# Output tiles at the end of a slot, and the exponentials' bias on ScalarE

## The reference

```python
q = hidden_states @ _dequant(q_codes, q_scales)
k = hidden_states @ _dequant(k_codes, k_scales)
v = hidden_states @ _dequant(v_codes, v_scales)
...
q = _rope(q)
k = _rope(k)
k = jnp.repeat(k, rf, axis=1)
v = jnp.repeat(v, rf, axis=1)
scores = jnp.einsum('bhqd,bhkd->bhqk', q, k) * scale + mask[None, None]
attn = jax.nn.softmax(scores, axis=-1)
out = jnp.einsum('bhqk,bhkd->bhqd', attn, v)
out = out.transpose(0, 2, 1, 3).reshape(b, s, NH * HD)
return out @ _dequant(o_codes, o_scales)
```

## Time and profile before

| what | us |
|---|---|
| median of 3 runs | 1576.78 |
| lowest and highest of them | 1571.9, 1584.11 |
| the profiled execution | 1574.17 |
| its span in the profile | 1572.4 |

### The profile page before, as it was taken

The page is one execution under the profiler, slowest core; times in us unless marked ns, Lnnn a source line. Parts: engine busy times, 40 slices in busy tenths (PEclk is TensorE's granted clock), DMA queues, the critical chain, the costliest instruction groups (busy, mean ns, idle before and its releaser), DMA issues.

```text
span 1572.4 us, 40997 instructions
## 1 busy us (share of the span) xinstructions
PE 1443.0 (92%) x11104; PEld 852.1 (54%) x11104; DVE 1294.1 (82%) x2884; ACT 926.2 (59%) x2198; POOL 935.1 (59%) x642
## 2 busy tenths in 40 slices
PE   4778899999999999999999999999999976999998
PEld 2445555556655555555565555556555553544543
DVE  7866689998889898889988999899889885776744
ACT  2465566667667666666667666666666762322421
POOL 2566677777777776777777777777777752110100
PEclk8989899999999999999999999999999987999999
DMA  8379988889889889988888888888988774010000
GB/s 265 61 165 178 166 154 158 158 157 165 158 156 162 155 160 155 167 154 161 158 171 162 163 161 155 161 160 161 166 158 156 142 130 91 14 54 29 26 28 27
DMA packets 522616, 217.15 MB, mean 138 GB/s; under 512 B 478944, under 2 KB 480704, under 8 KB 522432
## 3 DMA queue, kind: packets, MB, share of 16 engines
q1 hardware_dynamic: 519968, 210.53, 70.0%
q0 software_dynamic: 2464, 4.23, 1.5%
HBM read 55.32 MB, written 4.19 MB: 38 GB/s over the span
## 4 chain that ended last, share of the span: by engine, by line
PE 41%; issue 15%; DVE 11%; SPq 11%; DMA 10%; POOL 6%; ACT 4%; DVEq 2%; POOLq 0%; ACTq 0%
DMA ot<-o_parts 6%; DVE prob L1127 4%; SPq L384 4%; PE ps_s L1023 4%; PE ps_s L1024 4%; POOL p_lo L504 4%; PE ps_p L812 3%; PE ps_p L813 3%; PE ps_p L788 3%; PE ps_p L790 3%; PE ps_p L789 3%; DMA swap<-other 2%; PE ps_p L1037 2%; PE ps_p L1038 2%; DVE y L1114 2%
## 5 line engine op out<-in xcount | busy, mean ns | idle before, releaser
L504 POOL TENSOR_TENSOR p_lo<-prob,p_hi 128x1280 f16<-128x1280 f32 x128 | 340.7, 2661 | 175.8 <-ACT p_hi L633 155.5
L1114 DVE SCALAR_TENSOR_TENSOR y<-ps_p,wo_scale,y 128x512 f32<-128x512 f32 x512 | 380.8, 745 | 53.3 <-PE ps_p L813 31.6
L624 ACT ACTIVATE prob<-prob,exp_bias 128x512 f32<-128x512 f32 (+3 forms) x512 | 283.1, 553 | 164.7 <-DVE exp_bias L1136 164.3
L812 PE MATMUL ps_p<-ot,wo 128*128 128x512 f16 x512 | 199.5, 390 | 74.6 <-DMA ot<-o_parts 59.8
L788 PE MATMUL ps_p<-x_hi,w_hi 128*128 128x512 f16 x640 | 245.3, 383 | 5.5 <-DVE w_lo L1048 3.4
L789 PE MATMUL ps_p<-x_lo,w_hi 128*128 128x512 f16 x640 | 244.9, 383 | 0.0
L790 PE MATMUL ps_p<-x_hi,w_lo 128*128 128x512 f16 x640 | 244.7, 382 | 0.0
L1127 DVE CUSTOM_DVE_ANT_0 prob<-ps_s,mask 128x512 f32<-128x512 f32 (+3 forms) x512 | 237.0, 481 | 8.4 <-PE ps_s L827 7.3
L841 PE MATMUL ps_o<-v_hi,ffn_w 128*128 128x128 f16 x1280 | 222.6, 220 | 11.6 <-DVE rot L1102 11.0
L488 POOL TENSOR_TENSOR rot<-rot,swap 128x512 f32<-128x512 f32 x160 | 202.4, 1273 | 46.1 <-DMA swap<-other 45.8
L842 PE MATMUL ps_o<-v_lo,ffn_w 128*128 128x128 f16 x1280 | 222.4, 220 | 0.0
(11 more groups left out here) (100 smaller groups left out, 2979.7 us busy)
## 6 DMA issues: line engine op xcount, KB each, us to landing
swap<-other SPq DMA_DIRECT2D x320, 128.0 KB, 3.0
w_code<-w_codes SPq DMA_DIRECT2D x36, 384.0 KB, 3.7
w_scale<-w_scales SPq DMA_DIRECT2D x36, 384.0 KB, 4.9
o_code<-o_codes SPq DMA_DIRECT2D x35, 256.0 KB, 3.1
swap<-x SPq DMA_DIRECT2D x16, 256.0 KB, 2.8
out<-z SPq DMA_DIRECT2D x16, 256.0 KB, 2.0
ffn_w<-x SPq DMA_DIRECT2D x3, 1024.0 KB, 9.8
ffn_w<-p_hi SPq DMA_TRANSPOSE x128, 3.6
```

What stands on the lines that cost most here:

```text
L504: pool.tensor_tensor(p_lo[:, :], prob[:, hp, :], p_hi[:, :], ALU.subtract).then_inc(p_lod, 1)
L624: act.activation(prob[:, hp, a:a + w], prob[:, hp, a:a + w], ACT.Exp, bias=exp_bias[:, hp, i:i + 1], scale=-1.0, accum_out=exp_sum[:, hp, ...
L812: pe.matmul(ps_p[:, bank, :], w, flat(ot[:, hp, 0:TT, :]), start=True, stop=False)
L1114: dve.scalar_tensor_tensor(tile, ps_p[:, bank, :], scale, tile, ALU.mult, ALU.add).then_inc(o_add, 1)
```

## The change

Three things. The four output tiles of a slot go behind all scores and all pieces, on PE and on DVE, and V goes ahead of Q2. The bias is made by ACT, one instruction for each group of scores, ahead of that group's exponentials, with a wait for its own result. On POOL rope_add moves ahead of o_low, and on ACT v_high moves ahead of the last group of exponentials. Lines of the changed kernel are numbered a little differently (output tiles 818 and 819, attend 847 to 849).

```diff
-FULL = (("K",), ("Q0", "Q1"), ("Q2", "V"), ("Q3",))
+FULL = (("K",), ("Q0", "Q1"), ("V", "Q2"), ("Q3",))
...
-START = ("K", "Q0", "Q1", "Q2", "V", "Q3")
+START = ("K", "Q0", "Q1", "V", "Q2", "Q3")
...
 def slot_sequence(pieces):
-    return ("O0", "O1", "O2") + pieces + ("O3",)
+    return pieces + ("O0", "O1", "O2", "O3")
...
             def exps(n, hp, g):
+                first, count = min(GROUPS[g]), len(GROUPS[g])
+                act.wait_ge(low_done, n * TT + DONE[g])
+                act.activation(exp_bias[:, hp, first:first + count], low[:, hp, first:first + count], ACT.Copy,
+                               bias=EXP_UP).then_inc(bias_done, 1)
+                act.wait_ge(bias_done, n * NG + g + 1)
                 for i in GROUPS[g]:
                     a, w = P_AT[i], (i + 1) * P
-                    act.wait_ge(bias_done, n * NG + g + 1)
...
                     if more:
-                        scores(*nxt, 0)
-                    out_tile(n, h, 0)
-                    if more:
-                        scores(*nxt, 1)
-                    out_tile(n, h, 1)
-                    if more:
-                        scores(*nxt, 2)
-                    out_tile(n, h, 2)
+                        for g in range(NG):
+                            scores(*nxt, g)
                     for piece in slots[h]:
...
-                    out_tile(n, h, 3)
+                    for nt in range(KT):
+                        out_tile(n, h, nt)
...
                         if more:
                             lows(n + 1, hp, g)
-                            bias(n + 1, hp, g)
-                        out_tile(h, g)
...
                     for V, vpar, piece, bank, taken in made(U, r, h, slots):
-                        if piece != "V":
-                            take(V, vpar, piece, bank, taken)
-                    out_tile(h, 3)
-                    for V, vpar, piece, bank, taken in made(U, r, h, slots):
-                        if piece == "V":
-                            take(V, vpar, piece, bank, taken)
+                        take(V, vpar, piece, bank, taken)
+                    for nt in range(KT):
+                        out_tile(h, nt)
```

More of the change, by code:

```diff
@@ L541, in unit @@
                     p_low(n, h % 2)
+                    roped = [x for x in made_before(U, r, h, slots) if x[2] != "V"]
+                    if first and h == 0:
+                        start_rope("Q3")
+                    else:
+                        for V, vpar, piece, bank, taken in roped:
+                            rope_add(V, vpar, piece, taken)
                     if not (first and h < 2):
@@ L544, in unit @@
                     if first and h == 0:
-                        start_rope("Q3")
                         rope_low(0, 0, "Q3")
                     else:
-                        roped = [x for x in made_before(U, r, h, slots) if x[2] != "V"]
-                        for V, vpar, piece, bank, taken in roped:
-                            rope_add(V, vpar, piece, taken)
                         for V, vpar, piece, bank, taken in roped:
@@ L663, in _ @@
             rope_high(0, 0, "K")
+            v_high(0, 0, START.index("V") % 2, START.index("V") + 1)
             xt_high(2)
@@ L669, in _ @@
             o_centre(0)
-            v_high(0, 0, START.index("V") % 2, START.index("V") + 1)
             rope_high(0, 0, "Q1")
@@ L708, in unit @@
                                 rope_high(V, vpar, piece)
+                    for V, vpar, piece, bank, taken in made(U, r, h, slots):
+                        if piece == "V":
+                            v_high(V, vpar, bank, taken)
                     if more:
@@ L711, in unit @@
                         p_high(n + 1, (h + 1) % 2)
-                    for V, vpar, piece, bank, taken in made(U, r, h, slots):
-                        if piece == "V":
-                            v_high(V, vpar, bank, taken)
                     for piece in slots[h]:
@@ L1129, in lows @@
                                              accum_out=low[:, hp, i:i + 1]).then_inc(low_done, 1)
[L1131 to L1137, removed]
             def invert(n, h):
@@ L1172, in _ @@
                 lows(0, 0, g)
-                bias(0, 0, g)
             start_piece(5)
```

## The result

| | us |
|---|---|
| before, median of 4 runs | 1574.93 (1571.9 to 1584.11) |
| after, median of 4 runs | 1667.31 (1659.32 to 1671.28) |
| ratio, 95% interval | 1.057 [1.051, 1.063] |
| profiled execution after, its span | 1667.43, 1665.6 |

The account below looks back on a forecast made before the run. PE, busy 92%, was taken to bound the kernel. The unit was to grow from 38.24 to 40.02 us, +50 over 28 units, start -5, so 1574 + 45 = 1619 us; range 1572 to 1652.

Parts of the forecast that it names:

- I credit the whole 58 us: Steady part on PE: the new order gives back 58 of the 70 us lost to waits.
- O3's bank wait: Fourth output tile of every slot waits 0.6 us for the last piece's PSUM bank, 2.4 us a unit.
- The V chain: Slot 2: V's bank frees late, behind swaps, rope_adds, q_hi, v_hi and v_lo; 12.34 us instead of 10.30, 2.04 lost.
- rival A: Only the four fourth-tile bank waits count, the V chain is hidden: unit 38.6, total 1579 us; chance 0.25.
- a sign that it is wrong: Slot 2: the prediction is wrong if q_hi of Q1 ends before 8 us of the slot.
- rival B: Slot 2: V chain keeps its old times or DMA gets worse, 3.1 us lost, unit 41.1, total 1649; chance 0.15.
- The loop's turn, 12 us: Attend where PE's loop turns over, every four units: 12 us of the 70, 0.43 a unit, left alone by the change.
- Rival D: TensorE's clock: if two waits of slot 2 brought it down, more than rival B is lost; chance 0.04.
- w_low hidden by attend and the scores: Start of slot 0 on DVE: w_low of 2.90 us stands ahead of the lows, hidden since the scores take 3.3 us.
- I count nothing more: DVE without the bias: 183 us, 1.43 a slot, off the path; PE's 7.8 + 1.8 us waits are already in the 58.
- ACT's bias hidden: 384 small ACTIVATEs on ACT, 1.2 us a slot, 154 us at full price, hidden except 0.4 us in the round.
- Start -5, end 0: Before the steady part, waits for ot go and seven slots pay 0.6 each, about -5 us; the 18.2 us end stays.

Follow-up runs that it names:

- e3: Changed kernel with v_high ahead of the q_hi and k_hi on ACT; 1627.36 us, 1.033 of the kernel before.
- e4: Changed kernel with the first output tile ahead of the pieces on PE and DVE, three tiles behind them; 1574.01 us, 1.000 of the kernel before.
- e6: e3 with the first output tile ahead of the piece in slot 3 alone; 1609.59 us, 1.021 of the kernel before.
- e1: Kernel before with only the bias moved to ACT, old order kept; 1539.15 us, 0.977 of the kernel before.
- e2: Changed kernel with the bias back on DVE, so the new order alone; 1644.1 us, 1.044 of the kernel before.
- e5: Changed kernel with the edits of both e3 and e4; 1545.62 us, 0.982 of the kernel before.
- e11: e5 with PE's loop written as three rounds of eight units and four more written out, so fewer turns; 1547.73 us, 0.983 of the kernel before.
- e7: e5 with DVE's w_low in slot 2 behind the second output tile, not at the end of slot 3; 1548.74 us, 0.984 of before.

## Why the prediction was wrong

By its own steps, each against its measurement.

- **"I credit the whole 58 us" of removed waits, and O3's bank wait at 0.6 us in every slot.** Both right. The waits for ot are gone; 113 waits for rot of 0.48 us on average in the view, and slots without another wait take 8.19, 10.87 and 10.96 us in slots 3, 1 and 2, which is 0.57, 0.66 and 0.66 above the slots without a wait. e3 shows slot 2 alone with it, and e4 shows it gone when one tile moves.
- **The V chain, 2.04 us over in slot 2.** Right in mechanism, and in size only in the mean: the 28 slots 2 took 12.24 us in the mean (12.06 without the first, of 17.16), 12.34 was forecast. They are of two kinds. Ten take 10.96 or 10.97 us, the bank wait alone, as rival A had it; in these the q_hi of Q1 is done before 8 us, which the prediction had named as a sign that it is wrong. Three more take 11.35 to 11.94. The other fifteen take 12.17 to 13.93 us, the first of them 17.16, up to and beyond the 13.4 of rival B. All thirteen shorter ones lie in the first two units of a round of PE's loop. No run shows why the chain is early there, so that the mean came out as forecast is in part luck.
- **The loop's turn, 12 us, "and the change leaves the loop alone": this step failed.** Already before, the sum had it too small: the six slots 3 with the turn took 10.30 us in the mean, 2.7 over the 7.62, 16 us in all. And the loop's code is the same in the changed kernel, but what stands ahead of it isn't. A slot 3 with the turn at its end and the slot 0 after it took 12.35 and 9.90 us in the mean (one such pair goes from 806.55 over 818.91 to 828.49), where 8.22 each were forecast. That is 5.8 us a turn, 35 in six, and the sum had 12: 23 us too few. The idle time named "issue" is 24.0 of the 35, and the lower clock behind the turns some 10. e4 and e6 show that the bank wait ahead of it is what makes the turn longer: without it the idle time is 2.2 and 2.4 us a turn, not 4.0.
- **Rival D, the clock, at 0.04 and without a price.** It came true together with the forecast, not in place of it: 20 to 22 us, about half of it behind the turns, half behind the two waits of slot 2, which is where the rival had looked for it.
- **"w_low hidden by attend and the scores": failed in every fourth unit.** The three output tiles that stood ahead of K, 1.3 us, were part of its cover and are gone. PE waits up to 1.3 us for w_lo (1.7 us in all before), and seven slots 0 take 9.77 us instead of the forecast 8.22: 11 us.
- **"I count nothing more" for DVE's loss of the bias, and ACT's bias hidden: failed in both directions.** Alone it gives 35 us (e1), because p_hi, turn_o and the swaps follow DVE's lows; in the new order it costs about 20 us (e2), because ACT's part delays the V chain (first swap by 0.9 us, v_hi by 1.2). Its own figure for DVE was short too (179 us of busy time gone, 125 forecast), and that for ACT long (58 us more, 75 or more forecast). Each wait was put down to the engine named in it, and a DMA that comes last was taken as a matter of the DMA. The Trainium skill, Perfetto Trace Analysis, Optimizing Scalar/DVE Operations, which says that giving work of a saturated DVE to ScalarE may make sense, was set aside for the engine at 82%: the old order bears it out with 35 us, not with the 183 that the prediction worked out for it.
- **Start -5, end 0.** Start -4.0, end +5.4. The first output tiles of the end wait 11.9 us behind y of ACT, a line that wasn't there.

The balance, 47 of the 48 us between 1619 and the profiled 1667: 23 for the turns and their clock, 11 for w_lo, 7 for six slots 3 of 9.2 to 9.8 us that ran in part at the lower clock, behind a slot 2 in which PE had waited for v_lo, 6 for start and end, 1 for the other slots 0; slots 1 and 2 together are 1 us under the forecast.

The mistake behind the failed steps was in the form of the sum: it priced the turn and w_lo as the kernel before had them, and left out that a new wait just ahead of a loop's end makes the turn longer, and that tiles moved away take their cover with them.

## What to carry to other kernels

Before tiles are moved, count how many entries of the PSUM rotation follow the last piece in its slot: with four banks, as here, the fourth entry must have something long ahead of it, and one tile of each slot moved (e4) was worth 93 us with all that hung on it. Look at what stands ahead of a loop's end on TensorE: a semaphore wait that is still open there went with a turn of 4 us, its absence with one of 2. And a wait named after a DMA may end late because of a compute engine three steps back: follow it to the first step that waits for nothing, since DVE's small instructions were worth 35 us although hardly any wait bore DVE's name.

## What the runs showed of the hardware

**At a loop turn TensorE was idle for about 4 us behind an open bank wait, about 2 us without one.** 24.0 us in six cases in the changed kernel, 13.0 and 12.4 in e4 and e5. DVE has stops of 0.9 to 2.3 us of its own (e11), near the start of a round of its loop. The Trainium skill, Runtime: NRT & Kernel Launch, Instruction fetch mechanics, says that a taken branch to a page that isn't held stalls the engine for a fetch; idle time with "issue" as its reason fits that, though no run here shows the fetch itself.

**The clock.** It fell to the 1.2 GHz level behind the 4 us of a turn, and also in a slot 2 with two waits, as the first three lines, of the changed kernel, show. In e4 (the last two) it fell behind one wait of 2.48 us, with no other near it:

```profile
268.03 0.39 PE L818 MATMUL ps_p<-ot,wo 128*128 128x512 f16 x1 [2.31 <-DVE v_lo L1092]
269.23 0.60 PE L818 MATMUL ps_p<-ot,wo 128*128 128x512 f16 x1 [0.59 <-DVE rot L1103]
...
268.70:272.00 3.30, 2.77 (x21) 2.23 (x22) 3.02 (x5) 0.76 (x1) 2.90 (x2) 0.50 0.69 139
...
261.13 0.39 PE L818 MATMUL ps_p<-ot,wo 128*128 128x512 f16 x1 [2.48 <-DVE v_lo L1093]
...
261.50:264.80 3.30, 3.30 (x32) 3.11 (x30) 2.66 (x5) 1.06 (x1) 2.90 (x2) 0.50 0.79 157
```

The length of the wait doesn't decide it by itself. The same pair with 2.03 and 0.59 us (764.40 and 765.60, above) left it at 2.4 GHz, and a pair with 1.64 and 0.59 us (at 598.17) brought it down. In before, e1 and e5 waits of up to 2.3 us never did in the steady part, while it fell behind 1.96 us in e4 (at 414.43), behind a turn of 2.34 us in e7 and behind 1.99 and 2.66 us in e11. What decides, these runs don't show.

**DVE's product is stretched by about the time that POOL works beside it.** Timelines of the kernel before, one case, and the group at 175.7 us, where POOL was idle:

```profile
518.04 2.62 POOL L504 TENSOR_TENSOR p_lo<-prob,p_hi 128x1280 f16<-128x1280 f32 x1 [1.02 <-DMA ot<-o_parts]
...
L1058 DVE SCALAR_TENSOR_TENSOR w_scale<-w_code,w_scale x1: 950/950/950, 175.7 to 175.7; 128x768 f32<-128x768 int32 x1
```

The product that started at 519.61 took 1.87 us: until 520.66, when p_lo ended, and then 0.82 more. In the changed kernel POOL waits for the swaps at that time and the product takes 0.95 us in nearly every unit. That is 47 of the 179 us (79.1 us in 32 instructions before, 32.1 after) that DVE lost in busy time. The Trainium skill, SBUF — State Buffer, SBUF: two separate sides, describes the ports that DVE and GpSimd share as an exclusive lock for the length of an instruction; the trace agrees, 1.05 us of overlap for 0.92 us of stretch. It can go the other way too: the last product in the changed kernel (1334.25) took 0.95 us beside POOL's pair of rope_adds, and the pair took 3.36 us instead of 2.50.
